# A transformer layer with linear attention: a quarter of W1 corrected on GpSimd, three orders changed, the last attention product in other banks

## What is computed

```python
xn = layernorm(x)
q, k, v = split(xn @ qkv_w + qkv_b)          # 16 heads
q = l2norm(q); k = l2norm(k)
kv = einsum('bhnd,bhne->bhde', k, v)         # no softmax
attn = einsum('bhnd,bhde->bhne', q, kv).reshape(b, n, c) @ proj_w + proj_b
ffn = relu(xn @ W1 + b1) @ W2 + b2           # 256 -> 1024 -> 256
return x + attn + ffn
```

## Time and profile before

| what | value |
|---|---|
| time, median of 3 runs | 557.82 us (557.75 to 557.85) |
| the profiled execution | 558.1 us, of which the span is 556.3 |
| PE busy | 550.9 us, 99% of the span |
| DVE busy | 412.7 us, 74% |
| ACT busy | 284.8 us, 51% |
| POOL busy | 116.8 us, 21% |
| TensorE clock granted | 1.0 of full speed, mean |

### The profile page before, as it was taken

How to read it: one execution, slowest core, us unless ns; L and a number is a source line. 1 busy time by engine, 2 the same in 40 slices (tenths; PEclk the granted TensorE clock), 3 DMA queues, 4 the chain that set the end, 5 groups by cost and what they waited for, 6 DMA issues and landing times.

```text
span 556.3 us, 8972 instructions
## 1 busy us (share of the span) xinstructions
PE 550.9 (99%) x2724; PEld 467.1 (84%) x2724; DVE 412.7 (74%) x810; ACT 284.8 (51%) x518; POOL 116.8 (21%) x148
## 2 busy tenths in 40 slices
PE   8999999999999999999999999999999999999997
PEld 7888888888888888888888888888888888888896
DVE  6887889677785867859667686876778777783755
ACT  4676474556435663375644556445554555533421
POOL 3242422402052020520214202231024301150100
PEclk9999999999999999999999999999999999999999
DMA  8422135244423434034341343314333251313412
GB/s 259 158 87 49 27 85 96 69 96 96 91 42 85 98 86 97 19 87 97 86 89 28 86 97 86 80 35 111 73 91 67 45 106 38 81 34 82 106 39 77
DMA packets 141414, 45.36 MB, mean 82 GB/s; under 512 B 133330, under 2 KB 136402, under 8 KB 141396
## 3 DMA queue, kind: packets, MB, share of 16 engines
q1 hardware_dynamic: 139280, 44.61, 34.7%
q10 hardware_dynamic: 2116, 0.53, 0.5%
HBM read 20.98 MB, written 8.39 MB: 53 GB/s over the span
## 4 chain that ended last, share of the span: by engine, by line
PE 89%; ACT 3%; DVE 3%; DMA 2%; issue 1%; SPq 1%; POOL 0%; DVEq 0%; POOLq 0%; ACTq 0%
PE o_bank L1102 11%; PE o_bank L1101 11%; PE o_bank L1100 11%; PE w_bank L1100 10%; PE w_bank L1101 10%; PE w_bank L1102 10%; PE v_bank L1100 6%; PE v_bank L1102 6%; PE v_bank L1101 6%; PE g_bank L1102 3%; PE g_bank L1101 3%; PE g_bank L1100 3%; DMA w_raw<-w 2%; PE kv_bank L1255 1%; ACT qk_sq L550 0%
## 5 line engine op out<-in xcount | busy, mean ns | idle before, releaser
L572 ACT ACTIVATE h_hi<-w_bank 128x512 fp32r<-128x512 f32 x128 | 76.4, 597 | 64.7 <-PE w_bank L1102 64.4
L896 DVE SCALAR_TENSOR_TENSOR h_lo<-w_bank,h_hi 128x512 fp32r<-128x512 f32 x128 | 87.3, 682 | 28.0 <-ACT h_hi L572 26.5
L1100 PE MATMUL w_bank<-xT_hi,w_hi 128*128 128x512 f32 x254 | 100.1, 394 | 0.2 <-DVE h_lo L896 0.2
L1101 PE MATMUL w_bank<-xT_lo,w_hi 128*128 128x512 f32 x254 | 99.2, 391 | 0.0
L1102 PE MATMUL w_bank<-xT_hi,w_lo 128*128 128x512 f32 x254 | 98.9, 389 | 0.0
L1100 PE MATMUL o_bank<-h_hi,w_hi 128*128 128x512 f32 x240 | 93.4, 389 | 0.0
L1102 PE MATMUL o_bank<-h_hi,w_lo 128*128 128x512 f32 x240 | 93.4, 389 | 0.0
L1101 PE MATMUL o_bank<-h_lo,w_hi 128*128 128x512 f32 x240 | 93.4, 389 | 0.0
L394 POOL TENSOR_TENSOR xn_lo<-xn,xn_hi 128x256 fp32r<-128x256 f32 x56 | 41.5, 741 | 218.5 <-ACT xn_hi L498 214.2
L409 POOL TENSOR_TENSOR y_sb<-y_sb,y_rows 128x256 f32<-128x256 f32 x56 | 52.2, 937 | 125.2 <-DVE y_rows L935 103.1
L550 ACT ACTIVATE qk_sq<-v_bank 128x512 f32<-128x512 f32 x64 | 38.3, 598 | 70.5 <-PE v_bank L1102 69.4
(11 more groups left out here) (203 smaller groups left out, 983.5 us busy)
## 6 DMA issues: line engine op xcount, KB each, us to landing
y_rows<-blocks SPq DMA_DIRECT2D x256, 32.0 KB, 1.9
x_sb<-x SPq DMA_DIRECT2D x15, 512.0 KB, 3.8
y_sb<-x SPq DMA_DIRECT2D x60, 128.0 KB, 3.0
out<-y_sb SPq DMA_DIRECT2D x58, 128.0 KB, 2.5
xT_raw<-blocks SPq DMA_DIRECT2D x224, 32.0 KB, 1.9
y_sb<-w SPq DMA_DIRECT2D x4, 256.0 KB, 5.6
x_sb<-x SPq DMA_DIRECT2D x2, 256.0 KB, 2.9
w_raw<-w SPq DMA_DIRECT2D x2, 256.0 KB, 7.9
```

The lines of the kernel that those rows point to most:

```text
L572: nc.scalar.activation(h_hi[:, j % RING, :], w_bank[j % 2][:], ACT.Relu).then_inc(h_done, 1)
L896: nc.vector.scalar_tensor_tensor(h_lo[:, r, :], w_bank[j % 2][:], 0.0, h_hi[:, r, :].bitcast(F32), ALU.max, ALU.subtract).then_inc(h_lo_do ...
L1100: nc.tensor.matmul(to, left[0], right[0], start=first, stop=False, skip_group_check=shared)
L1101: nc.tensor.matmul(to, left[0], right[1], start=False, stop=False, skip_group_check=shared)
```

## The change

Four edits, none within the loop over batches 1 to 6:

1. **Part 1 of W1.** PE no longer sums it in `kv_bank`, which takes four fp32 products from its opening (eight records of the profile). It forms the correction alone there (`raise_by`, one product of 256 columns), ACT copies that to SBUF, in tile 0 of xn_first (`second_raise`), and POOL adds it to the part in SBUF, a 128x512 addition. ACT's high part and DVE's low part of it are made from SBUF, ahead of `h_high(0, 0)` and `h_low(0, 0)`.
2. **Orders of the opening.** ACT takes `w2_high(1)` behind `h_high(0, 2)` and `w1_high(2)`, and `h_high(0, 3)` ahead of the high part of wqk. DVE takes `w1_low(2)` ahead of raising wqk and `h_low(0, 3)` ahead of `wqk_lo`. POOL's `w2_low(0)` and `w2_low(1)` get one more wait each.
3. **Half 1 on DVE.** `h_low(1, 2)` goes ahead of `norms(1)`; `k_low` and `h_low(1, 3)` go ahead of `divide q`.
4. **Last attention.** It goes to `w_bank[0]` and `v_bank[1]`, and waits for seven `h_low` of the half, not eight.

```diff
--- before.py
+++ after.py
@@ -151,10 +151,12 @@
         g_bank = bank("g_bank")
         kv_bank = bank("kv_bank")
+        last_banks = [w_bank[0], v_bank[1]]
         first_banks = [o_bank, [g_bank, kv_bank]]
         pair_banks = [o_bank, [g_bank, w_bank[1]]]
-        w1_sum = [v_bank[0], kv_bank]
-        w1_raise = [None, None, g_bank[:, 2 * P:4 * P], v_bank[1][:, 0:2 * P]]
+        w1_sum = v_bank[0]
+        w1_raise = [None, kv_bank[:, 0:2 * P], g_bank[:, 2 * P:4 * P], v_bank[1][:, 0:2 * P]]
+        second_raise = xn_first[:, 0, :]
         kv_raw = kv_bank[:].rearrange("p (g w n) -> p g w n", g=KC, w=2)
@@ -445,14 +448,21 @@
                                         channel_multiplier=-1).then_inc(const_set, 1)
             def opening():
+                second = part_columns(1)
+                pool.wait_ge(second_raise_copied, 1)
+                pool.wait_ge(w1_loaded[1], 16)
+                nc.gpsimd.tensor_tensor(w1_raw[second], w1_raw[second],
+                                        second_raise.unsqueeze(1).to_broadcast([P, KC, 2 * P]), ALU.add).then_inc(w1_second_raised, 1)
+
+
+                pool.wait_ge(w1_ready, 4)
                 w2_low(0)
                 pool.wait_ge(qkv_rows_loaded, 32)
                 less_first(slice(0, 2 * C))
+                pool.wait_ge(wqk_raised, 1)
                 w2_low(1)
                 pool.wait_ge(wqk_ready, 1)
                 less_first(slice(2 * C, 3 * C))
-
-
                 pool.wait_ge(ln_offset_done, 1)
                 w2_low(2)
                 w2_low(3)
@@ -596,9 +606,12 @@
             def w1_high(part):
                 cols = part_columns(part)
-                if part < 2:
-                    act.wait_ge(w1_summed, part + 1)
-                    raised_part = w1_sum[part][:].rearrange("p (k n) -> p k n", k=KC)
+                if part == 0:
+                    act.wait_ge(w1_summed, 1)
+                    raised_part = w1_sum[:].rearrange("p (k n) -> p k n", k=KC)
+                elif part == 1:
+                    act.wait_ge(w1_second_raised, 1)
+                    raised_part = w1_raw[cols]
                 else:
                     act.wait_ge(w1_raised, part - 1)
                     raised_part = w1_raw[cols]
@@ -614,24 +627,26 @@
             act.wait_ge(const_set, 2)
             nc.scalar.activation(unread[:], positive[:], ACT.Sqrt)
             ln_sqrt(0)
+            act.wait_ge(w1_raise_ready, 1)
+            copy(second_raise, w1_raise[1]).then_inc(second_raise_copied, 1)
             w1_high(0)
             xT_high_pair(0, 0)
             xT_high_pair(0, 1)
             xT_high_pair(1, 0)
             xT_high_pair(1, 1)
+            w1_high(1)
             w2_high(0)
-            w1_high(1)
             h_high(0, 0)
             def opening():
                 h_high(0, 1)
-                w2_high(1)
                 h_high(0, 2)
                 w1_high(2)
+                w2_high(1)
                 w1_high(3)
+                h_high(0, 3)
                 act.wait_ge(wqk_raised, 1)
                 copy(wqk_hi[:], wqk_raw).then_inc(wqk_hi_ready, 1)
-                h_high(0, 3)
                 h_high(0, 4)
                 ln_sqrt(1)
                 qk_out(0, 0, 0)
@@ -811,7 +826,7 @@
                 return nc.vector.tensor_tensor(weights, weights, by.unsqueeze(1).to_broadcast(list(weights.shape)), ALU.add)
             def raise_w1(part):
-                dve.wait_ge(w1_raise_ready, part - 1)
+                dve.wait_ge(w1_raise_ready, part)
                 dve.wait_ge(w1_loaded[part], 16)
                 raised(w1_raw[part_columns(part)], w1_raise[part]).then_inc(w1_raised, 1)
@@ -822,9 +837,8 @@
             def w1_low_chunk(j):
                 cols = chunk_columns(j)
-                dve.wait_ge(w1_hi_ready, j // 2 + 1)
-                raised_part = w1_sum[j // 2][:].rearrange("p (k n) -> p k n", k=KC)
-                less(w1_lo[cols], raised_part[chunk_columns(j % 2)], w1_hi[cols]).then_inc(w1_ready, 1)
+                dve.wait_ge(w1_hi_ready, 1)
+                less(w1_lo[cols], w1_sum[:].rearrange("p (k n) -> p k n", k=KC)[cols], w1_hi[cols]).then_inc(w1_ready, 1)
             def transpose_blocks(to, token_major, done):
                 for a in range(PAIRS):
@@ -921,7 +935,7 @@
                 wait(dve, o_ready, (2 * b * KC) + k + 1)
                 wait(dve, yT_copied, KC * 2 * b + k + 1)
                 to = by_tile(yT[0][:, k, :])
-                nc.vector.tensor_tensor(to, in_pairs((w_bank if last else v_bank)[k][:]), to, ALU.add).then_inc(yT_added, 1)
+                nc.vector.tensor_tensor(to, in_pairs((last_banks if last else v_bank)[k][:]), to, ALU.add).then_inc(yT_added, 1)
             def spread_y(b, u, k):
@@ -959,22 +973,21 @@
             xT_low_pair(1, 0)
             xT_low_pair(1, 1)
             w1_low_chunk(1)
+            w1_low(1)
             h_low(0, 0)
-            w1_low_chunk(2)
-            w1_low_chunk(3)
             def opening():
                 h_low(0, 1)
                 raise_w1(2)
                 raise_w1(3)
                 h_low(0, 2)
+                w1_low(2)
                 dve.wait_ge(qkv_raise_ready, 1)
                 dve.wait_ge(wqk_loaded, 16)
                 raised(wqk_raw, qkv_raise[:, 0:2 * C]).then_inc(wqk_raised, 1)
-                w1_low(2)
+                h_low(0, 3)
                 dve.wait_ge(wqk_hi_ready, 1)
                 less(wqk_lo[:], wqk_raw, wqk_hi[:]).then_inc(wqk_ready, 1)
-                h_low(0, 3)
                 row_stats(1, 0, 1)
                 moments(1)
                 spread(1)
@@ -1009,9 +1022,9 @@
                 sum_squares(1, 3)
                 bound(1)
                 xT_low(2, 0)
+                h_low(1, 2)
                 norms(1)
                 divide(1, 1, k_done)
-                h_low(1, 2)
             def half(b, s, u, last):
                 ahead = not (last and u == 1)
@@ -1019,13 +1032,14 @@
                     if ahead:
                         xT_low(s + 1, 1 - u)
                     h_low(s, 2)
+                if is_second(s):
+                    k_low(s, u)
+                    h_low(s, 3)
                 divide(0, u, q_done)
                 if not is_second(s):
                     transpose_q(s, u)
                     h_low(s, 3)
-                k_low(s, u)
-                if is_second(s):
-                    h_low(s, 3)
+                    k_low(s, u)
                 if not last:
                     variance(s + 2, b + 1, u)
                 h_low(s, 4)
@@ -1108,22 +1122,17 @@
                 return nc.tensor.matmul(to, raise_signs[0:raise_row + 2], raise_rows[:, first:first + to.shape[1]], start=True, stop=True)
-            def part_of_sum(part, k):
-
-
-                return w1_sum[part][:, k * 2 * P:(k + 1) * 2 * P]
-
-            def spread_part(part):
-                first = part * 2 * P
-                for k in range(KC):
-                    nc.tensor.matmul(part_of_sum(part, k), raise_signs[0:raise_row + 2], raise_rows[:, first:first + 2 * P],
+            def raise_first_part():
+
+
+                sums = [w1_sum[:, k * 2 * P:(k + 1) * 2 * P] for k in range(KC)]
+                for k in range(KC):
+                    nc.tensor.matmul(sums[k], raise_signs[0:raise_row + 2], raise_rows[:, 0:2 * P],
                                      start=k == 0, stop=False, skip_group_check=True)
-
-            def raise_part(part):
-                first = part * 2 * P
-                pe.wait_ge(w1_loaded[part], 16)
-                for k in range(KC):
-                    done = nc.tensor.matmul(part_of_sum(part, k), ident[:], w1_raw[:, k, first:first + 2 * P],
+                raise_by(w1_raise[1], 2 * P).then_inc(w1_raise_ready, 1)
+                pe.wait_ge(w1_loaded[0], 16)
+                for k in range(KC):
+                    done = nc.tensor.matmul(sums[k], ident[:], w1_raw[:, k, 0:2 * P],
                                             start=False, stop=k == KC - 1, skip_group_check=True)
                 done.then_inc(w1_summed, 1)
@@ -1298,10 +1307,7 @@
             pe.wait_ge(rows_loaded, 32)
             pe.wait_ge(raise_rows_cleared, 1)
             pe.wait_ge(const_set, 4)
-            for part in range(2):
-                spread_part(part)
-            for part in range(2):
-                raise_part(part)
+            raise_first_part()
             transpose_pair(0)
             raise_by(w1_raise[2], 4 * P).then_inc(w1_raise_ready, 1)
             transpose_pair(1)
@@ -1341,8 +1347,8 @@
                         ffn_up(s + 1, 1 - u, j + AHEAD - JC)
                     ffn_down(s, b, u, j, last)
                     if j == 5 and not ahead:
-                        pe.wait_ge(h_lo_done, JC * (s + 1))
-                        attend(b, 0, w_bank)
+                        pe.wait_ge(h_lo_done, JC * (s + 1) - 1)
+                        attend(b, 0, last_banks)
                     if j == 1 and ahead:
```

(1 more changed line is left out.)

## The result

| kernel | median | lowest to highest | runs |
|---|---|---|---|
| before | 557.64 us | 556.84 to 558.17 | 20 |
| after | 558.88 us | 558.71 to 559.48 | 20 |

The time lies inside the range of 8 in 10 and outside the forecast's own, 557.2 to 558.1, and the sign is the other one. The profiled execution after took 558.78 us, span 557.0; that of before, on which I argued, took 558.1, 0.46 us above the median of its kernel, which turns out to matter.

What follows compares the result with a forecast made beforehand. A DVE, ACT and POOL chain beside PE until 72.5 us, then PE alone, was taken to bound it. 558.1 + 0.1 - 0.25 = 557.95, less 0.28 for the median 557.67, stated as 557.6; range 556.5 to 559.0.

Steps and rivals of the forecast that it cites:

- The lead out of the opening: Opening: new orders bring normalise from 25.07 to 23.9, and in half 1 k_low comes 1.07 earlier.
- first addition ahead, second held: Opening, column 0: DVE's first small addition precedes POOL's, the second is held to about 9.2 to 9.35; cost 0.
- The 0.28 that I took off for the median: Final sum: the median of the runs is 0.28 below the profiled execution, so 557.95 becomes 557.67.
- The 8.3: Opening: without the four products PE's first transposes could begin about 8.3 where they began at 8.75, 0.45 free.
- Half 1: Half 1 on DVE: k_low 1.07 earlier, divide q behind it +1.17, so ln_offset and ffn_up(7) +0.1.
- The race I feared: Half 1: variance's small instruction loses to POOL's wv_lo, +1.3 at ffn_up(7), 558.95 to 559.7; chance 0.16.
- The rival: Opening: DVE's first small addition is held by POOL's; the chain loses 0.8 of its 1.2, 558.45; chance 0.22.
- The tail: Last attention, at 544.10: the stall of 0.25 goes, -0.25.
- The lead kept: Rival: divide q slips between POOL's tiles, h_low(1, 4) comes 1.1 earlier, gain 1.2 to 1.4, 556.5; chance 0.18.

Runs made afterwards that it cites:

- the second trace of before: The kernel before, unchanged, timed and profiled again against itself: ratio 1.0002, span 555.9 us, W2's second part there by 14.1.
- The version without both causes: Changed kernel with POOL's addition waiting for both small additions and half 1 in the order of before: median 556.71, ratio 0.9984.
- taking two more holds off its chain: Late addition, half 1 as before, POOL's value-weight split waiting for half 3's variance, projection-weight split for its ln_offset: median 556.53, ratio 0.9987.
- the split addition: Changed kernel with POOL's addition of W1's second part as two instructions of 128x256: median 558.65, ratio 1.0022.
- the trace with `divide q` back: Changed kernel with divide q back ahead of k_low in half 1, nothing else undone: median 557.94, ratio 1.0009.
- with the cast out of the way: Late addition, half 1 as before, POOL's cast of the value weights waiting for half 3's variance: median 556.68, ratio 0.9990.

## Why the prediction was wrong

**The lead out of the opening: the step that failed.** The sum had `divide q`'s +1.17 paid for by a lead: normalise from 25.07 to 23.9, and so `k_low` 1.07 earlier. After, normalise stood at 24.71 and `k_low` at 58.29, 0.36 and 0.21 earlier, so `ln_offset` and `ffn_up(7)` came 0.84 later, not 0.1. The lead failed in two places.

First, "first addition ahead, second held. Cost 0". The first small addition was held for 0.94, the transposes began at 9.04 and not at 8.3, and normalise follows the transposes by 15.67. With POOL's addition late and nothing else changed the chain came out as I had worked it out: transposes at 8.08, raise of wqk at 16.45 (forecast 16.6), normalise at 23.75 (23.9), `k_low` at 57.35 (57.43), `ffn_up(7)` at 72.35 (72.55), and the profiled execution took 557.85 against the 557.95 of the sum. This step is worth 0.93 at `ffn_up(7)` and 0.85 in the medians.

Second, even that kernel is slower than before, 1.0014, since the lead was one over a single execution. Of the 1.32 by which its normalise is ahead of 25.07, 0.67 is the earlier start of the transposes, and 0.65 is W2's late landing, which the chain of the earlier trace rows shows and the second trace of before does not have; there the distance is 15.68 with the old orders. Against the usual execution of before the new orders win next to nothing, and half 1's +1.1 stands alone. The 0.28 that I took off for the median hid this: I took the changed kernel to be as far below its profiled time as before is, but its median, 558.88, is 0.10 above it.

Timeline of ACT, after:

```profile
23.74 0.60 ACT L560 ACTIVATE qk_sq<-v_bank 128x512 f32<-128x512 f32 x1 [0.20 <-PE v_bank L1116]
24.23 0.59 ACT L508 ACTIVATE qk_even<-v_bank 128x512 f32<-128x512 f32 x1
24.71 2.07 ACT L526 ACTIVATE xn_first<-x_sb,ln_offset,ln_rstd 128x256 f32<-128x256 f32 x4
```

Normalise comes directly behind the q and k of tile 0, and these wait for PE. I had followed DVE's gain to it without looking at them. Here that cost little: DVE's `ln_offset` ended at 24.64, just ahead of it, and from transposes at 8.3 PE's pace gives 23.97, about my 23.9. That the two limits lie so close together is luck of the forecast, not something it had worked out. The 8.3 itself was too careful: without the hold the transposes began at 8.08, directly behind the column that was ready at 8.03.

**Half 1: the mechanism and the price were right.** I had `divide q` cost 1.17 behind `k_low`. From `k_low` to `ln_offset` it was 9.07 in the first trace of before and 10.12 after: +1.05, with the 1.13 idle in the trace and 1.0010 and 1.0029 in the runs with that order on the kernel before. That `variance` meets POOL's tiles and the cast as before held for two of three instructions: L795 took 0.60 and L797 0.57 after, against 0.64 and 0.57 of the same instructions before, but the sum of the row ahead of them (L776 before, L791 after) took 0.17 where it had been held to 0.52. L800 was not caught. The race I feared did not happen.

**The hold.** I took "first addition ahead, second held" and argued with POOL's reaction to a semaphore. POOL was ahead in all three traces with its addition unguarded, at 7.70, 7.15 and 7.25. The row of the addition names the landing of W1's second part, not a reaction of POOL, as what ended its wait, and I had read the time of that landing off one execution. The rival's price was right: 0.8 forecast, 0.93 measured at `ffn_up(7)`. Before anything is taken off for the median, my rival gives 558.1 + 0.1 - 0.25 + 0.8 = 558.75, and the profiled execution took 558.78. Its 558.45 missed the median of 558.88 by that step from one execution to the median.

**The tail.** I had 0.25; from the last product ahead to the second matmul of the attention it was 0.60 and is 0.36. From `ffn_up(7)`, +0.84 between the two first traces, to PE's last matmul, +0.59, the difference is 0.25. Right.

**The lead kept.** It did not come about: `divide q` had to be paid. The version without both causes is another kernel; it came to 556.71, near the 556.5 that I gave for this rival, and taking two more holds off its chain won no time that can be told.

Left open: what the addition on POOL is worth in itself. In the seven traces of kernels with the sum on PE the transposes began at 8.08 to 8.88. In five of them the timeline names no wait of PE for a landing, and the four products into v_bank ahead (L1119 in the kernel before) took 1.03 to 1.91 for the same work, at a granted clock of 1.00 in each, the higher of its two levels; why is not shown. In the other two PE waited for W1's second part, and the transposes began at 8.75 and 8.70. In the four traces with the late addition they began at 8.00 to 8.36, though those products took 1.05 to 1.88 there. That fits the narrow 556.51 to 556.97 against the two groups of the kernel without the addition, but which opening goes with which time was seen in one trace each and is not shown.

## What to carry to other kernels

Where two engines can hold each other and less than 0.1 us decides which comes first, the better outcome is not worth its full price: here it was entered at cost 0, came out the other way in each of the three traces with that race, and took 0.9 us. Take the chain from two executions when a transfer is on it; the first may be the exception, and a gain over it is then no gain over the kernel. Before adding up a gain along a chain of waits, look at what stands just ahead of each instruction on its own engine, since a gain lasts only to the next instruction that is released from elsewhere. And an instruction moved out of a gap leaves the gap empty: here the same 1.13 us of work was free between two waits and cost all of it behind them.

## What the runs showed of the hardware

Some instructions of DVE and POOL cannot run together, and they hold each other both ways, in the order in which they start: L822 was held 0.94 by POOL's addition, and POOL's four tiles took 4.22 for 3.18 with `divide q` among them. Not every instruction is held: beside the late addition (POOL, 1.28 from 8.95) two DVE subtractions of 128x256 that read a bank and one tile took 0.76 from 8.97, as they did before with POOL idle. The Trainium skill, page "SBUF — State Buffer", section "Who interferes with whom", says that whoever issues first gets the shared pair for the whole instruction; the split addition agrees, with one hold per half, 0.42 and 0.40. New to me was that the 128x256 normalising instruction, 0.41 us long and with a value per partition for both of its scalars, is held as well: 1.37 us in the trace with `divide q` back, where I had counted on the small additions alone. And a hold removed is not yet time won: with the cast out of the way the chain was caught by a later POOL instruction, for 0.62 (0.78 where 0.16 is usual).
